# Copying quantised activations straight to the shifted copies from two queues, instead of by a plane in DRAM

## The reference, cut to what matters

```python
def qrelu(x):
    return jnp.clip(ste_round(jnp.clip(x, 0.0, 10.0) / RELU_SCALE), 0.0, 255.0) * RELU_SCALE
...
out00 = bconv(x, 0)                                  # 3x3 convolution with weights of +-scale
x_b0l1 = qhtanh(out00) + qhtanh(op0)
out01 = bconv(qrelu(x_b0l1), 1)
...
out10 = bconv(x_b1l0, 2)                             # x_b1l0 is a qrelu too
...
out11 = bconv(x_b1l1, 3)                             # x_b1l1 is a qrelu too
```

## Time and profile before

| | |
|---|---|
| median of 3 runs | 4374.5 us (4368.3 to 4380.27) |
| the profiled execution, its time | 4387.05 us |
| its span | 4385.2 us |
| PE busy | 4187.6 us, 95% of the span |
| DVE, ACT, POOL busy | 2945.6, 1831.5, 3077.7 us |
| granted TensorE clock, mean | 0.983 of full |

### The profile page before, as it was taken

How to read it: one execution, slowest core, us unless ns; L and a number is a source line. 1 busy time by engine, 2 the same in 40 slices (tenths; PEclk the granted TensorE clock), 3 DMA queues, 4 the chain that set the end, 5 groups by cost and what they waited for, 6 DMA issues and landing times.

```text
span 4385.2 us, 67257 instructions
## 1 busy us (share of the span) xinstructions
PE 4187.6 (95%) x24997; PEld 2015.3 (46%) x24997; DVE 2945.6 (67%) x6076; ACT 1831.5 (42%) x2008; POOL 3077.7 (70%) x3094
## 2 busy tenths in 40 slices
PE   2899999999999999999999999999999999999993
PEld 2444444444444544444454444444444454444441
DVE  5656677667766766777677767766776676666553
ACT  1343444444444434444444444444444443444431
POOL 1777777777776767767777776777767677776740
PEclk8999999999999999999999999999999999999996
DMA  4677787878877787887878878787787878778762
GB/s 109 217 245 230 234 263 224 259 229 247 257 239 232 237 248 247 244 251 230 249 240 250 260 233 255 224 259 228 242 258 231 249 237 251 247 243 251 224 194 63
DMA packets 480252, 1022.94 MB, mean 233 GB/s; under 512 B 262164, under 2 KB 298356, under 8 KB 475636
## 3 DMA queue, kind: packets, MB, share of 16 engines
q1 hardware_dynamic: 311668, 474.56, 35.8%
q10 hardware_dynamic: 69984, 342.81, 23.7%
q0 software_dynamic: 98304, 201.52, 16.1%
HBM read 862.19 MB, written 73.20 MB: 213 GB/s over the span
## 4 chain that ended last, share of the span: by engine, by line
PE 81%; POOL 5%; DMA 5%; DVE 5%; issue 2%; SPq 2%; ACTq 1%; ACT 0%; POOLq 0%; DVEq 0%
PE ps_r L1489 58%; PE ps_y L1501 6%; PE ps_c L1475 6%; POOL ring L600 5%; PE ps_a L1428 3%; DMA taps_c<-plane_act 3%; PE ps_c L1515 2%; PE ps_a L1475 1%; PE ps_y L1522 1%; PE ps_a L1466 1%; DMA plane_act<-act_c 1%; PE ps_c L1570 1%; DVE work_c L1271 1%; PE ps_c L1548 1%; ACTq L790 1%
## 5 line engine op out<-in xcount | busy, mean ns | idle before, releaser
L600 POOL DMA_INDIRECT ring<-patch_table,idx_part x3072 | 3069.5, 999 | 1153.9 <-issue 1001.5
L1489 PE MATMUL ps_r<-select,image 128*128 128x512 f32 x6912 | 3151.4, 601 | 14.1 <-DVE col_hat L1195 9.5
L1489 PEld LDWEIGHTS ps_r<-select,image 128*128 128x128 f32 x6912 | 1259.6, 191 | 1401.6 <-issue 1383.6
L1195 DVE TENSOR_TENSOR col_hat<-ps_r,col_hat 128x512 f32<-128x512 f32 x1152 | 793.0, 688 | 1219.4 <-PE ps_r L1489 1215.1
L650 ACT ACTIVATE select<-row_in,minus_row 128x1536 f32<-128x1536 f32 x384 | 604.6, 1575 | 994.4 <-PE ps_r L1489 615.9
L652 ACT ACTIVATE select<-select,one_col 128x1536 f32<-128x1536 f32 x384 | 605.4, 1577 | 12.5
L669 ACT COPY samples<-ps_c 128x512 f32<-128x512 f32 x256 | 148.8, 581 | 638.3 <-PE ps_c L1515 638.1
L1501 PEld LDWEIGHTS ps_y<-col_hat,w_dense 128*32 128x32 f32 x9216 | 228.2, 109 | 291.1 <-issue 289.5
L1501 PE MATMUL ps_y<-col_hat,w_dense 128*32 128x128 f32 x9216 | 331.2, 277 | 0.0
L1204 DVE TENSOR_TENSOR ps_w<-ring,ps_w 128x384 f32<-128x384 f32 x512 | 284.5, 556 | 40.2 <-DMA ring<-patch_table,idx_part 35.9
L1210 DVE TENSOR_TENSOR ring<-ring,ps_w 128x384 f32<-128x384 f32 x512 | 279.9, 547 | 4.4
(11 more groups left out here) (231 smaller groups left out, 2414.6 us busy)
## 6 DMA issues: line engine op xcount, KB each, us to landing
row_in<-coord_table ACTq DMA_DIRECT2D x384, 768.0 KB
col_hat<-coord_table SPq DMA_DIRECT2D x384, 768.0 KB
ring<-patch_table,idx_part POOLq DMA_INDIRECT x3072
taps_c<-plane_act SPq DMA_DIRECT2D x135, 268.1 KB
coord_table<-wino SPq DMA_DIRECT2D x64, 216.0 KB
taps_c<-xn_c ACTq DMA_DIRECT2D x96, 130.0 KB
taps_c<-xn_c SPq DMA_DIRECT2D x96, 130.0 KB
plane_act<-act_c SPq DMA_DIRECT2D x180, 65.0 KB
```

The source lines that it names most:

```text
L600: nc.gpsimd.indirect_dma_start(out=ring[j][:, h % 2, k, :], out_offset=None, in_=table, in_offset=bass.IndirectOffsetOnAxis(ap=idx_part[:, ...
L1195: v.tensor_tensor(hat_t, ps_r[:, (s + t) % 2], hat_t, ALU.mult).then_inc(tile_weighed, 1)
L1489: ins = mm(ps_r[:, (s + t) % 2], image[:, m, t], select[s % 2][:, m], start=(m == 0), stop=(m == PAIRS - 1))
```

## The change

The plane in DRAM is given up. Every image now does what only the last one did: in slots 6, 9 and 12 SP issues six direct copies (`copy_taps`) and ACT issues the other six (`share_copies`), after each has waited for the `relu` event. SP's wait for the stored plane and its three loads in slots 7, 10 and 13 go. PE waits for all twelve copies (`COPIES_IN`). In the first 15 images this is 45 times.

```diff
                 if s == 3:
                     sp.wait_ge(c_dve.sem, c_dve.at(n, "norm2"))
                     copy_taps(taps_c[:], xn_c, taps_c_in)
-                if s in (7, 10, 13) and not last_image(n):
-                    i = (s - 7) // 3
-                    sp.wait_ge(plane_out, n * (PLANE_OUT * (CONVS - 1)) + PLANE_OUT * (i + 1))
-                    load_taps(taps_act, plane_act, taps_act_in)
                 if s in (6, 9, 12):
                     sp.wait_ge(c_dve.sem, c_dve.at(n, f"relu{(s - 6) // 3}"))
-                    if known_zero(n) and s == 6:
-                        sp.wait_ge(planes_cleared, 16 * 2)
-                    if last_image(n):
-                        copy_taps(taps_act, act_c, taps_act_in)
-                    else:
-                        store_plane(plane_act, act_c, plane_out)
+                    copy_taps(taps_act, act_c, taps_act_in)
...
-                if s in (6, 9, 12) and last_image(n):
+                if s in (6, 9, 12):
                     act.wait_ge(c_dve.sem, c_dve.at(n, f"relu{(s - 6) // 3}"))
                     share_copies(taps_act, act_c, taps_act_in)
...
-                    pe.wait_ge(taps_act_in, n * ((CONVS - 1) * TAPS_IN) + (COPIES_IN if last_image(n) else TAPS_IN) * i)
+                    pe.wait_ge(taps_act_in, (n * (CONVS - 1) + i) * COPIES_IN)
```

More of the change, by code:

```diff
@@ L181, in build @@
         coord_table = nc.dram_tensor("coord_table", [1 + 2 * ITEMS, ROWS * HALF], F32).ap()[1:, :]
-        plane_act = nc.dram_tensor("plane_act", [C, XG + 2], BF16)
         ident = sb("ident", [P, P])
@@ L282, in build @@
         halo_c = sem("halo_c")
-        planes_cleared = sem("planes_cleared")
-        plane_out = sem("plane_out")
         taps_a_in = sem("taps_a_in")
@@ L385, in copies @@
                 yield dst[dx * C:(dx + 1) * C, lo - dx:hi - dx], src[s * C:(s + 1) * C, lo - s * RS * XW:hi - s * RS * XW]
-        def last_image(n):
-            return isinstance(n, int) and n == N - 1
         n_weight_dmas = 0
@@ L413, in copy_taps @@
                     sp.dma_start(to, frm).then_inc(done, 16)
[L415 to L424, removed]
             load_x(0)
@@ L435, in _ @@
             sp.wait_ge(zeroed, 4)
-            for lo in (0, 1 + XW + STRIPS * RS * XW):
-                sp.dma_start(plane_act.ap()[:, lo:lo + 1 + XW], act_c[0:C, 0:1 + XW]).then_inc(planes_cleared, 16)
             def load_later():
@@ L1613 @@
 PREP_DVE = 3
-PLANE_OUT = STRIPS * 16
-TAPS_IN = SHIFTS * 16
 COPIES_IN = SHIFTS * STRIPS * 16
```

## The result

The changed kernel takes 4539.3 us (median of 4 runs, 4536.05 to 4540.61), the kernel before 4376.8 us beside it (4 runs). The ratio is 1.0369, with a 95% interval of 1.0353 to 1.0384. The prediction was 4555 us. The profiled execution took 4540.01 us, 153.0 more than the one of before.

What follows compares the result with a forecast made beforehand. PE, busy 95% of the span, bounds the kernel. Waits 3.6 + 4.4 plus clock 5.2 give 13.2 us an image, 198 over 15, less 17: +181, 4568 us profiled, median 4555; range 4510 to 4605, with rivals 4470 to 4620.

Steps and rivals of the forecast that it cites:

- Removed, 17 us: Trip through DRAM: PE's 14.2 us of waits for the plane go, plus 2.9 us of slowed clock; lower bound 0.
- Added on SP, nothing: SP's six issues replace four; SP is held some 2 us longer, which the slots cover, so nothing is counted.
- Six issues, 4.2 us: ACT's queue in slots 6, 9 and 12: six direct copies take 4.2 us, between bounds of 3.98 and 5.60.
- From the last issue to the select, 1.03 us: ACT's queue: 1.03 us from the end of the issues to the select's start, including the load of `row_in`.
- Select(8) in time: Behind `relu0`, select(8) is ready at 2034.2 and PE wants it at 2035.19: no wait, at most 0.4 us.
- Late loads of `row_in`: ACT's loads behind the copies move later, but select(12) is covered by 6 us, so no further wait.
- The clock, 5.2 us an image: PE's matmuls slow behind the two waits for select, costing 2.5 and 2.7 us, together 5.2 (3.4 to 5.7).
- PE's lost time is lost: PE's waits and slow clock lengthen the whole run: 6.6 us lost across a 3.75 us wait, nothing made up.
- the clock didn't hold: Rival: PE's clock holds, so waits come without the 5.2 us; +106 us, 4480 us; chance 0.15.
- the issues were not cheap: Rival: ACT's issues are cheap where other work runs, only the plane's waits go; -17, 4357 us; chance 0.03.
- the late loads made no further waits: Rival: late loads of `row_in` make more PE waits, issues costing 5.6 us; +260, 4635 us; chance 0.14.
- the loss is far over 13 us: Rival: nothing to measure, within 13 us, because new waits replace other waits of PE; chance 0.03.

Runs made afterwards that it cites:

- sp_only: Changed kernel with all twelve direct copies issued by SP, ACT issuing none and not waiting for relu; 4375.5 us, 0.998 of the kernel before.
- only6: Changed kernel with ACT issuing six copies in slot 6 only, SP all twelve in slots 9 and 12; 4371.8 us, 0.9962 of the kernel before.
- act_late: Changed kernel with ACT's six copies issued right after the select of slots 7, 10 and 13; 4361.5 us, 0.9951 of the kernel before.
- act_late5: Same kernel as act_late, timed in more rounds; 4364.2 us, 0.9964 of the kernel before.
- wait_only: Kernel before, plane kept, with ACT waiting for relu at the end of slots 6, 9 and 12 but issuing nothing there; 4495.7 us, ratio 1.0251.
- act3: Changed kernel with SP issuing nine direct copies and ACT three, at the same places; 4436.9 us, 1.0114 of the kernel before.
- only9: Changed kernel with ACT issuing six copies in slot 9 only, SP all twelve in slots 6 and 12; 4461.1 us, 1.0167 of the kernel before.
- only12: Changed kernel with ACT issuing six copies in slot 12 only, SP all twelve in slots 6 and 9; 4460.6 us, 1.0164 of the kernel before.

## Why the prediction was right

The time, 4539.3, lies 16 us under the 4555 forecast and in the range; the likeliest case was the one that came, by the mechanism that it names. An image took 270.7 us (from 2163.62 above to the same wait one image later, 2434.34), where 273 was forecast and 259.8 was usual before. By its steps:

- **Removed, 17 us.** Right. The plane's waits are gone. sp_only, only6, act_late and act_late5 show gains of 0.2 to 0.5%.
- **Added on SP, nothing.** Right for the steady state; an issue costs 0.63 us there, more than the 0.47 of a store in the earlier trace rows, and no one waits for it.
- **Six issues, 4.2 us.** Measured 4.08 and 4.03. The nearer bound, the last image's, was the right one to lean on.
- **From the last issue to the select, 1.03 us.** Measured 0.75 to 0.77. The load of `row_in` takes 0.61 us behind bfloat16 copies, and took 0.89 behind float32 ones. This and the 0.12 us of the step above made both waits some 0.4 us too long: 3.6 and 4.4 forecast, 3.17 and 3.92 measured; 15 x 0.9 = 14 us of the difference to the profiled sum.
- **Select(8) in time.** Right: only6. In the changed kernel it is ready at 2093.41 and PE wants it at 2089.94 + 5.33 = 2095.27, which is 1.9 us of room, where 1.0 was forecast.
- **Late loads of `row_in`.** The load behind `relu1` was issued at 2124.51, and select(12), which waited for it, started at 2133.65, 9.1 us later (8.6 forecast). It was ready at 2136.84, and PE wanted it at 2141.57. No further wait came of it in the changed kernel. wait_only shows that a similar delay is dear with the plane; that the direct copies bear it because they are one transfer and not two in a row is likely, but not shown.
- **The clock, 5.2 us an image.** PE's busy time grew by 61.8 us; with the 2.9 that the removed wait had cost, 65 / 15 = 4.3 us. The step was over by 0.9 us an image, 13 us in all. The mean hides a spread: the price of one wait ran from 1.3 to 2.7 us (last section).
- **PE's lost time is lost.** Right: the account above closes within 1 us.

Where luck helped: by its steps the forecast was further off than the median shows. The profiled execution was forecast at 4568 and took 4540, 28 us less, of which the waits make 14 and the clock 13. The forecast median is only 16 us off because 12.55 us were taken off for the profiled execution of before, which lay that far above its median; that of the changed kernel lies 0.7 us above its own.

The rivals fell: the clock didn't hold, the issues were not cheap, the late loads made no further waits, and the loss is far over 13 us. On the page that spoke against the forecast, "DMA: Bandwidth & Descriptors" of the Trainium skill: its 50 ns for a dispatch stand in "Anatomy of one DMA", which is about DMAs issued by GpSimd, a limit that the prediction left out. They can't be carried over to these issues: 0.63 us each on SP (sp_only), 0.67 to 0.71 on ACT (changed kernel, act3). In "Issuing engines are not separate DMA queues", the time to initiate is called "usually small relative to the DMA itself". No run here shows how long one of these copies takes, so that is neither borne out nor refuted; the loss came from what stood behind the issues, whatever their share of the copy.

## What to carry to other kernels

A DMA issue is an instruction of the engine that makes it: here 0.6 to 0.7 us each for these copies, plus the wait ahead of the first. Before sharing copies with a compute engine, find what stands behind them in its order, arithmetic and loads both, and who waits for that. Putting the same six issues behind the next `select` turned a loss of 3.7% into a gain of 0.4%.

## What was not expected of the hardware

**The price of one wait in clock differs for the same wait.** Behind 3.17 to 3.2 us, always at the same tile, the next six matmuls took 4.12 us in one image of the changed kernel and 5.49 in most images of only9, where 2.84 is usual. In the changed kernel the waits of slot 14, 3.9 us each, were followed by 4.4 to 4.5 and 5.5 us, in turn from image to image. In only12 three of the 15 waits of slot 14, 3.9 us long as well, were followed by 2.84 us, which is no price at all. The stretches behind these two waits (columns as in the earlier trace rows, the granted clock third from the end), first of the changed kernel, then of only9:

```profile
2128.00:2130.00 2.00, 1.54 (x4) 0.83 (x5) 0.00 (x0) 0.40 (x1) 1.57 (x2) 0.97 1.06 387
2130.00:2132.00 2.00, 2.00 (x4) 0.48 (x2) 0.00 (x0) 0.00 (x0) 1.52 (x2) 0.50 1.03 294
2132.00:2134.00 2.00, 2.00 (x28) 1.25 (x28) 1.28 (x3) 0.35 (x1) 1.39 (x3) 0.68 1.00 297
```

```profile
2090.00:2092.00 2.00, 1.81 (x2) 0.84 (x3) 0.00 (x0) 0.13 (x1) 1.39 (x3) 0.50 1.06 383
2092.00:2094.00 2.00, 2.00 (x4) 0.91 (x3) 0.00 (x0) 0.00 (x0) 1.70 (x2) 0.50 1.00 265
2094.00:2096.00 2.00, 2.00 (x10) 0.48 (x13) 0.22 (x1) 0.00 (x0) 1.39 (x3) 0.50 1.00 264
```

In the first the clock stays up until PE is at work again and falls then, in the second it is at the 1.2 GHz level from the start. In act3 the matmuls were slow behind 5 of the 15 waits of slot 14 (1.96 to 2.05 us) and behind 2 of the 15 of slot 11 (1.53 and 1.23 us); behind all others, though as long, they took 2.84 us. What decides it for one wait stays open here.

**An issue is no cheaper when one queue issues alone.** SP alone, with twelve in a row, needs 0.63 us each (sp_only). In the changed kernel, while ACT issues six beside it, SP needs 3.77 us for its six behind `relu1`, which is 0.63 us each as well, and ACT 4.08 / 6 = 0.68.
